# Another order of the projected tiles in a fused gated-delta-rule and feed-forward block

## The chip, the cores and the metric

The kernel runs on one core of one Trainium2 chip. The metric is the device time of one execution in microseconds (us). The kernel before takes 1098.72 us, the median of three runs (1098.14 to 1103.36).

## What is computed

Four sequences of 512 tokens, width 512. Each half is modulated by a condition (layer norm, scale, shift, gate). The first half is a gated delta rule with 6 heads (key 64, value 128), the second a SiLU-gated feed-forward of 2048. All in f32.

```python
h = _layernorm(x) * (1 + ca) + sa
q = short_conv(h @ Wq, conv_wq)      # 384 columns; conv over 4 tokens, then silu
k = short_conv(h @ Wk, conv_wk)      # 384 columns
v = short_conv(h @ Wv, conv_wv)      # 768 columns
beta = sigmoid(h @ Wb); g = -exp(A_log) * softplus(h @ Wa + dt_bias)
# per token: S = S*exp(g); S += k (v - k S) beta; o = q S
o = o * rsqrt(mean(o*o) + EPS) * norm_weight * silu(h @ Wg)   # gate: 768 columns
x = x + ga * (o @ Wo)
x = x + gb * ffn(_layernorm(x) * (1 + cb) + sb)
```

## The kernel before, in words

The host-side code first writes a plan, a list of steps in one order; each engine then walks that list and issues its own part of every step, so all engines share the plan's order, and waits are semaphores. The stages are: norms and the projection of k (4 x 4 slots, to about 90 us); the projection of q, v and the output gate, beside which the inverses for the chunks are made (to about 338 us); a recurrence over 16 units (to about 540 us); the feed-forward.

The change is in the second stage. It has 15 tiles of 128 columns, three of q (numbers 0 to 2), six of v (3 to 8) and six of the gate (9 to 14); `tile_seq` is their order. Each tile is done for 4 batches, so there are 60 slots. In the prediction a projection or taps "of slot n" carry the slot's number, from 0. In slot n:

- TensorE first projects for slot n+1: 12 matmuls of 128x512, the f32 product being made of three products of float32r halves (L1258 is the helper that issues a matmul). It needs one of four PSUM banks, freed by the slot four before.
- At the first slot of a tile the next tile's weights are split: high part on ScalarE, difference ("weight difference") on VectorE (L1851 is the helper for all tensor_tensor operations), and the load of a later weight on SyncE's queue waits for that difference.
- q or v tile ("convolution slot"): `conv_in` on ScalarE scales the bank into one of two Y buffers; `conv_out` on ScalarE, one slot late, writes SiLU of Y into one of three output buffers O; three `conv_tap` operations on VectorE ("taps", L1956), of which the last frees the bank. Gate tile ("gate slot"): one SiLU on ScalarE from the bank into an O buffer, which frees the bank. `store_u` on SyncE's queue (L1131) stores O to `scrU` in DRAM.
- Then the side lanes put in their next steps. L1580 is the helper for every ScalarE activation.

The side lanes, with the steps that matter:

- `inverse_1`, from slot 4: per group of four units a table load, exponentials, a table load back; per unit a product k·k on TensorE and one VectorE operation (L2022), two copies on ScalarE, and four stores to `scrA` on SyncE (L1138).
- `inverse_2`, once all 16 units are planned: loads from `scrA` (L1148), then the substitution: 31 pairs of a multiply and an add on VectorE, each needing the one before; then stores to `scrP` (L1162), 16 loads back (L1169) that wait for these stores, and the P tiles being cleared on GpSimd (L2265). The lane makes three steps in a gate slot and at most two in a convolution slot.
- `q_norms`, from slot 21: loads of q, squares on ScalarE in slots 28 to 30, sums and turns on TensorE in slots 32 and 33.
- `merge`, once the loads back are planned: per unit 12 small products (merge_a), copies on ScalarE, transposes on VectorE (L2067), 12 more (merge_b) and copies on VectorE (L2056). TensorE's steps use two pairs of PSUM banks in turn.

In the kernel before the loads from `scrA` are in slot 15, the substitution in slots 17 to 41, the stores to `scrP` in slot 42, the loads back in slot 44, the merges in slots 46 to 55.

```python
            else:
                step("conv_in", j=3 + tile, bank=i, done=t, y=y, n=ys["n"], tap=tap)
                put_out()
                for k in range(3):
                    step("conv_tap", j=3 + tile, bank=i, y=y, tap=tap, d=k)
                left[1] = min(left[1], 2)
```

Of the kernel before, what the change touches and what calls it, by code (L numbers as in the profile page):

```python
# [53 lines left out]
def build(nc, x, W1, cw, dtb, alog, nw, Wo, cT, wmod, wg, cst, out):  # L54
# [212 lines left out]
        return ap.unsqueeze(axis).broadcast_to(shape)  # L267

    order = [s * 4 + b for b in range(4) for s in range(4)]
    tile_seq = [0, 9, 1, 10, 2, 11, 3, 12, 4, 13, 5, 6, 7, 8, 14]  # L270
    MODS = [0, 1, 3, 2, 4, 5]
    WSEQ = [0, 1, 2, 3] + [4 + n for n in tile_seq]

# [2134 lines left out]
```

How the kernel before makes its waits and increments, by code:

```python
    def all_posted(e):  # L1056
        e.wait_ge(sem("po_wo"), 16)
        e.wait_ge(sem("p_x1"), 16)
        e.wait_ge(sem("v_xn1"), 16)
        for n in range(2):
            e.wait_ge(sem(f"d_x1{n}"), 512)
# [17 lines left out]
    def sync(e):  # L1079
        def load_x(n):
            u = order[n]
            if n >= 5:
                e.wait_ge(sem("v_xn"), n - 4)
            e.dma_start(X[n % 5][:, :], x[u % 4, (u // 4) * 128:(u // 4) * 128 + 128, :]).then_inc(sem(f"d_x{n % 5}"), 16)
# [1 line left out]
        def load_mod(r):  # L1086
            i = MODS[r]
            if r >= 2:
                e.wait_ge(sem("mod_mm"), r - 1)
            if r == 0:
                e.dma_start(wm[0][:, 0:2, :], wmod[:, 0:2, i * 512:(i + 1) * 512]).then_inc(sem("d_wmh"), 16)
                e.dma_start(wm[0][:, 2:4, :], wmod[:, 2:4, i * 512:(i + 1) * 512]).then_inc(sem("d_wm0"), 16)
                return
            e.dma_start(wm[r % 2][:, :, :], wmod[:, :, i * 512:(i + 1) * 512]).then_inc(sem(f"d_wm{r % 2}"), 16)
# [1 line left out]
        def load_w(j):  # L1096
            if j >= 2:
                e.wait_ge(sem("v_wlo"), j - 1)
            e.dma_start(Wraw[j % 2][:, :, :], W1[WSEQ[j]]).then_inc(sem(f"d_w{j % 2}"), 16)
# [28 lines left out]
            elif kind == "store_u":  # L1128
                o, b = st["o"], st["b"]
                e.wait_ge(*at_least(st["act"]))
                e.dma_start(scrU.rearrange("(s b) p j t -> b j p s t", b=4)[b, st["tile"]],
# [2 lines left out]
                u = st["u"]  # L1134
                s, w = unit(u)
                e.wait_ge(sem("v_ab6"), u + 1)
                for k in range(4):
```

## Time and profile before

| | |
|---|---|
| median of three runs | 1098.72 us |
| profiled execution | 1101.88 us |
| its span, first to last instruction | 1099.9 us |
| mean granted TensorE clock | 0.983 |
| TensorE matmul / weight load busy | 95% / 77% |
| VectorE / ScalarE / GpSimd busy | 57% / 34% / 19% |
| projection of q, v, gate, with the inverses | about 90 to 338 us |

The profile is of one execution. Busy shares are means over stages with different limits. Matmuls overlap in the array and their ends are modelled, so that TensorE can seem busy where it runs with short waits. "PEld" is the weight load, "SPq" SyncE's queue of DMA issues. A value in brackets behind a row is the idle time of the engine ahead of it and what ended it. The granted clock is a share of 2.4 GHz.

### The profile page before, as it was taken

To read this page: it belongs to the slowest core of one execution; us is meant where nothing else is said; L and a number is where in the kernel's file an instruction comes from. 1 tells how busy PE (TensorE), PEld (TensorE's weight loads), DVE (VectorE), ACT (ScalarE), POOL (GpSimd) and SP (SyncE) were. 2 spreads that over 40 slices of the span, in tenths; PEclk is the share of its full clock that TensorE was granted. 3 is DMA by queue.
4 is the path that set the end of the run, shared out by engine and by line. 5 is a ranking of instruction groups with operands and counts; after the bars stand their busy time and mean duration, and the time that the engine had idled before them with its cause. 6 is when DMAs were issued, how large, how long until landed. Compare 5 with 4: busy or idle time off the path is not lost.

```text
span 1099.9 us, 18621 instructions
## 1 busy us (share of the span) xinstructions
PE 1046.9 (95%) x7356; PEld 844.7 (77%) x7356; DVE 632.2 (57%) x995; ACT 374.3 (34%) x685; POOL 207.8 (19%) x163
## 2 busy tenths in 40 slices
PE   5799999998989999999989999999999999999998
PEld 3675667777767788888777787888888888888886
DVE  6868355999774677787766333333333433434356
ACT  3476464353445333343355112121221211122110
POOL 1132200011014544544331000000000000004191
PEclk8899999999889999999999999999999999999999
DMA  6503235737519466666622000010010100001223
GB/s 218 181 10 119 69 79 155 214 96 197 97 49 228 93 143 136 158 166 139 207 79 77 1 1 29 29 33 25 1 57 1 58 1 29 29 1 67 77 77 115
DMA packets 153414, 97.34 MB, mean 89 GB/s; under 512 B 93552, under 2 KB 130672, under 8 KB 153200
## 3 DMA queue, kind: packets, MB, share of 16 engines
q1 hardware_dynamic: 153328, 96.16, 32.2%
q8 instruction: 59, 0.97, 0.4%
q14 instruction: 27, 0.22, 0.1%
HBM read 64.67 MB, written 31.46 MB: 87 GB/s over the span
## 4 chain that ended last, share of the span: by engine, by line
PE 77%; DVE 12%; issue 4%; ACT 2%; DMA 2%; SPq 2%; POOL 1%; DVEq 0%; ACTq 0%; POOLq 0%
PE ps L1258 73%; DVE t L1851 5%; DVE t L1956 3%; PE ps L1266 3%; ACT t L1580 2%; DVE t L1856 1%; PE ps L1463 1%; DMA t<-in_x 1%; DMA t<-scrA 1%; SPq L1138 1%; DVE t L1861 1%; SPq L1195 1%; POOL t L2244 0%; DMA t<-scrU 0%; DVE t L2056 0%
## 5 line engine op out<-in xcount | busy, mean ns | idle before, releaser
L1258 PE MATMUL ps<-t,t 128*128 128x512 f32 (+6 forms) x6488 | 995.4, 338 | 42.3 <-DVE t L1851 16.8
L1258 PEld LDWEIGHTS ps<-t,t 128*128 128x128 f32 (+4 forms) x6488 | 787.0, 166 | 227.4 <-issue 45.1
L1851 DVE TENSOR_TENSOR t<-ps,t 128x512 f32<-128x512 f32 (+4 forms) x306 | 208.2, 700 | 257.9 <-PE ps L1258 243.6
L1580 ACT ACTIVATE t<-t 128x512 fp32r<-128x512 f32 (+10 forms) x339 | 188.8, 578 | 326.8 <-DVE t L1851 201.5
L1851 DVE TENSOR_TENSOR t<-t,t 128x512 fp32r<-128x512 f32 (+15 forms) x212 | 166.9, 792 | 109.2 <-ACT t L1580 98.2
L1580 ACT ACTIVATE t<-ps 128x512 f32<-128x512 f32 (+5 forms) x202 | 108.9, 551 | 317.2 <-PE ps L1258 308.7
L2334 POOL TENSOR_TENSOR t<-t,t 128x512 f32<-128x512 f32 x16 | 22.4, 1401 | 375.2 <-DVE t L1851 373.1
L1956 DVE SCALAR_TENSOR_TENSOR t<-ps,t,t 128x511 f32<-128x511 f32 (+2 forms) x108 | 80.3, 747 | 8.9 <-ACT t L1580 6.1
L1266 PE MATMUL ps<-t,t 128*128 128x128 f32 (+1 forms) x388 | 54.7, 276 | 5.0 <-DVE t L1856 2.8
L1580 ACT ACTIVATE t<-ps,t 128x512 f32<-128x512 f32 (+2 forms) x93 | 54.5, 616 | 14.0 <-PE ps L1266 6.7
L1266 PEld LDWEIGHTS ps<-t,t 128*128 128x128 f32 (+1 forms) x388 | 43.1, 142 | 16.5 <-issue 5.3
L2313 POOL TENSOR_TENSOR t<-t,t 128x768 fp32r<-128x768 f32 x16 | 29.1, 1818 | 42.9 <-ACT t L1580 42.7
L2265 POOL MEMSET t<- 128x3072 f32 x4 | 10.7, 2671 | 124.8 <-PE ps L1258 97.5
L2319 POOL TENSOR_TENSOR t<-t,t 128x512 f32<-128x512 f32 x16 | 20.7, 1296 | 55.6 <-DVE t L1851 55.4
L1580 ACT ACTIVATE t<-t,t 128x1 f32<-128x1 f32 (+2 forms) x36 | 13.2, 368 | 52.8 <-DVE t L1863 51.5
L2337 POOL TENSOR_TENSOR t<-t,t 128x512 f32<-128x512 f32 x16 | 22.9, 1430 | 39.9 <-DMA t<-scrX 37.9
L1861 DVE BATCH_NORM_STATS2 t<-t 128x6 f32<-128x512 f32 x32 | 22.0, 689 | 10.3 <-DMA t<-in_x 8.5
L2244 POOL TENSOR_TENSOR t<-t,t 128x512 fp32r<-128x512 f32 x13 | 17.0, 1304 | 52.8 <-ACT t L1580 51.5
L1856 DVE TENSOR_SCALAR t<-t,t,t 128x512 f32<-128x512 f32 x32 | 25.1, 787 | 3.1 <-PE ps L1266 2.9
L1944 DVE SCALAR_TENSOR_TENSOR t<-ps,t,t 128x510 f32<-128x510 f32 (+1 forms) x24 | 17.8, 744 | 11.5 <-ACT t L1580 10.9
L2305 POOL TENSOR_TENSOR t<-t,t 128x768 f32<-128x768 f32 x16 | 23.6, 1472 | 2.7 <-POOL t L2319 2.4
L2255 POOL TENSOR_TENSOR t<-t,t 128x384 f32<-128x384 f32 x16 | 13.7, 858 | 52.3 <-PE ps L1258 32.8
(50 smaller groups left out, 236.7 us busy)
## 6 DMA issues: line engine op xcount, KB each, us to landing
scrU<-t SPq DMA_DIRECT2D x60, 256.0 KB, 3.2
t<-in_wf SPq DMA_DIRECT2D x16, 768.0 KB, 4.2
t<-scrU SPq DMA_DIRECT2D x32, 288.0 KB, 4.7
t<-scrU SPq DMA_DIRECT2D x32, 192.0 KB, 3.4
t<-in_wmod SPq DMA_DIRECT2D x5, 1024.0 KB, 6.2
t<-in_W SPq DMA_DIRECT2D x19, 256.0 KB, 3.0
t<-in_x SPq DMA_DIRECT2D x16, 256.0 KB, 4.3
t<-in_x SPq DMA_DIRECT2D x32, 128.0 KB, 2.8
```

The lines of the kernel that those rows point to most:

```text
L1258: return e.matmul(o, l, r_, start=start, stop=stop, skip_group_check=True)
L1266: return e.transpose(o, i, idn)
L1580: return e.activation(o, i, f, **kw)
L1851: return e.tensor_tensor(o, a, b, op)
L1856: return e.tensor_scalar(o, a, s1, s2, o1, o2)
L1861: e.bn_stats(st6[:, slot_, :], src).then_inc(sem(name + "bn"), 1)
L1956: e.scalar_tensor_tensor(yy[:, d + 1:SEQ], p_[:, 0:SEQ - d - 1], cwt[:, j, 2 - d:3 - d], yy[:, d + 1:SEQ], ALU.mult, ALU.add).then_inc(sem ...
L2305: signal(e.tensor_tensor(heads(Sg[:, :, :]), heads(S[:, 6 * pp:6 * pp + 6, :]), bc(decay, 3, [128, 2, 3, 128]), ALU.mult), "p_sg")
L2313: signal(e.tensor_tensor(OZl[:, :, :], OZ[:, :, :], OZh[:, :, :].bitcast(f32), ALU.subtract), "p_ozl")
L2319: signal(e.tensor_tensor(YB[u % 2][:, :], YB[u % 2][:, :], XB[u % 2][:, :], ALU.add), "p_x1")
L2334: signal(e.tensor_tensor(ya(b, s), ya(b, s), gbB[:, b, :], ALU.mult), "p_out")
L2337: signal(e.tensor_tensor(ya(b, s), ya(b, s), xo(b, s), ALU.add), "p_out")
```

## The change

One line of the plan is another. Tile numbers 0 to 2 are q, 3 to 8 v, 9 to 14 gate.

```diff
     order = [s * 4 + b for b in range(4) for s in range(4)]
-    tile_seq = [0, 9, 1, 10, 2, 11, 3, 12, 4, 13, 5, 6, 7, 8, 14]
+    tile_seq = [0, 9, 1, 2, 3, 10, 11, 12, 13, 4, 5, 6, 7, 8, 14]
     MODS = [0, 1, 3, 2, 4, 5]
     WSEQ = [0, 1, 2, 3] + [4 + n for n in tile_seq]
```

Slots 0 to 11 and 40 to 59 keep their tiles. Slots 12 to 19 are q2 and v3, slots 20 to 35 four gate tiles, slots 36 to 39 v4. As the substitution's lane makes three steps in a gate slot and two in others, its last step comes in slot 40 instead of 41; the stores to `scrP` come in slot 41 instead of 42, the loads back in slot 42 instead of 44, and the merges in slots 45 to 54 instead of 46 to 55. The loads of the weights follow the new order.

## Rows read from the trace of the kernel before

**Rows 1.** The page: busy time of TensorE and share of the span.
```profile
span 1099.9 us, 18621 instructions
...
PE 1046.9 (95%) x7356; PEld 844.7 (77%) x7356; DVE 632.2 (57%) x995; ACT 374.3 (34%) x685; POOL 207.8 (19%) x163
```

**Rows 2.** Chain of waits, 126 to 350 us: start, length, what.
```profile
175.94 3.17 DMA scrA<-t
...
180.02 7.26 DMA t<-scrA
...
246.09 24.77 PE ps L1258 x108
270.87 3.74 issue
```

**Rows 3.** Busy time by stretch: stretch, length, engines, clock, DMA share, GB/s.
```profile
187.30:246.00 58.70, 53.72 (x264) 40.56 (x262) 56.88 (x79) 25.26 (x51) 5.35 (x2) 1.00 0.53 152
```

**Rows 4.** Timeline of TensorE, 160 to 300 us: start, length, what, [idle before].
```profile
190.22 22.31 PE L1258 MATMUL ps<-t,t 128*128 128x512 f32 x96 [2.10 <-DVE t L1956]
213.42 3.06 PE L1258 MATMUL ps<-t,t 128*128 128x512 f32 x12 [0.89 <-DVE t L1956]
...
226.05 16.03 PE L1258 MATMUL ps<-t,t 128*32 128x512 f32 x104 [0.15 <-ACT t L1580]
...
274.61 1.49 PE L1258 MATMUL ps<-t,t 32*32 32x32 f32 x48 [3.74 <-issue]
...
283.17 8.42 PE L1258 MATMUL ps<-t,t 32*32 32x32 f32 x168 [0.48 <-ACT t L1580]
```

**Rows 5.** Busy time by stretch of one microsecond; the third number from the end is the clock.
```profile
274.00:275.00 1.00, 0.39 (x15) 0.42 (x17) 0.43 (x2) 0.00 (x0) 0.00 (x0) 0.60 1.27 150
...
280.00:281.00 1.00, 1.00 (x3) 0.76 (x3) 0.86 (x3) 0.00 (x0) 0.00 (x0) 0.50 0.68 89
...
295.00:296.00 1.00, 1.00 (x4) 0.81 (x3) 0.93 (x3) 0.00 (x0) 0.00 (x0) 0.50 0.48 131
```

**Rows 6.** Timeline of VectorE, 126 to 262 us.
```profile
144.19 2.32 DVE L1956 SCALAR_TENSOR_TENSOR t<-ps,t,t 128x511 f32<-128x511 f32 x3 [1.83 <-ACT t L1580]
...
149.27 2.31 DVE L1956 SCALAR_TENSOR_TENSOR t<-ps,t,t 128x511 f32<-128x511 f32 x3 [1.81 <-ACT t L1580]
...
173.18 0.56 DVE L2022 SCALAR_TENSOR_TENSOR t<-ps,t 128x384 f32<-128x384 f32 x1 [1.33 <-DMA scrA<-t]
...
261.37 0.54 DVE L1851 TENSOR_TENSOR t<-t,t 128x93 f32<-128x93 f32 x2
```

**Rows 7.** Timeline of ScalarE, slots 12 and 48.
```profile
162.69 1.28 ACT L1602 ACT_TABLE_LOAD   x1
163.99 1.64 ACT L1580 ACTIVATE t<-ps 128x384 f32<-128x384 f32 x4
...
285.72 0.62 ACT L1580 ACTIVATE t<-t 128x512 f32<-128x512 f32 x1
```

**Rows 8.** Timeline of the SyncE queue, 160 to 300 us.
```profile
172.44 3.94 SPq L1138 DMA_DIRECT2D scrA<-t  x8
...
179.16 1.29 SPq L1148 DMA_DIRECT2D t<-scrA  x3
...
262.61 2.19 SPq L1162 DMA_DIRECT2D scrP<-t  x3
...
269.03 11.15 SPq L1169 DMA_DIRECT2D t<-scrP  x16
```

**Rows 9.** VectorE's groups by form, 186 to 262 us: count, busy, mean ns.
```profile
L1851 DVE TENSOR_TENSOR t<-t,t 128x512 fp32r<-128x512 f32 x6 | 4.1, 685 | 0.0
...
L1851 DVE TENSOR_TENSOR t<-t,t 128x768 f32<-128x768 f32 x2 | 1.9, 958 | 0.1
...
L1851 DVE TENSOR_TENSOR t<-t,t 128x93 f32<-128x93 f32 x4 | 1.1, 276 | 5.2 <-DMA t<-scrA 5.1
```

**Rows 10.** DMA issues, 160 to 355 us: KB each, median us to landing.
```profile
scrU<-t SPq DMA_DIRECT2D x49, 256.0 KB, 3.2
```

## The prediction

> **What bounds the kernel now.** I read the page first, then the chain of waits of the projection stage, then the timelines of TensorE, VectorE, ScalarE and the SyncE queue there, and last the granted clock in stretches of one microsecond. The page puts the kernel on TensorE: 95% busy [rows 1]. Only order changes, and only in slots 12 to 39, so what can be won or lost is TensorE's waiting, and time at the lower clock, between about 150 and 340 us; everything behind shifts with it. A slot is one 128-column tile for one batch; there are 60. TensorE runs a slot's projection one slot ahead, and can run up to three ahead, for four banks.
>
> The chain shows what waited last, in this order [rows 2]. Early TensorE; then the SyncE queue that stores the inverse's blocks, a landing, and the load of the substitution's operand, done at 187.3. Then VectorE until 246; TensorE again, 24.77 us for nine projections, 2.75 each; then 3.74 us in which TensorE stands for the inverse's return from memory. In 187.3 to 246 VectorE is busy 56.88 of 58.70 us, but TensorE 53.72 [rows 3]. TensorE's waits are few: 2.10 before 190.22 and 0.89 before 213.42, with some 2 us more at two like places; it makes eight projections in 22.31 us, 2.79 each, while VectorE is behind [rows 4]. The four banks absorb most of VectorE's lateness.
>
> The clock: at the higher level (1.00, 2.4 GHz) until 274, 0.60 in 274 to 275, 0.50 (1.2 GHz) until 281 and then 1.00 again [rows 5]. It follows the 3.74 us wait. Some 6.8 us at half rate lose 3.4 us. It falls three times more, first at 295 [rows 5], some 3.4 us each, each losing 1.7; these follow slots with four small merges.
>
> **The change part by part.** Instructions, bytes and buffers are the same. Tiles q1, q2, v3 stand in slots 8 to 19, gates in 20 to 35, v4 in 36 to 39. Against before, slots 12-15 become convolution slots, 24-27 and 32-35 gates, 36-39 a convolution; 16-23 and 28-31 keep their kind (with other tiles). Between the arrival of the substitution operand and its last sum stand five convolution slots fewer: before 18, 19, 24-27, 32-35, 40, 41 and after 18, 19, 36-40.
>
> Step 1, the head. In slots with a convolution and two unit products, VectorE's taps start every 5.08 us (144.19 to 149.27) [rows 6]: taps 2.24 (2.32 with the overlap at their end), products 1.05, then on ScalarE the copies of the blocks (1.5) ahead of the next slot's scaling, then 0.72 to the taps. In gate slots before, unit 15 is done at 173.18 + 0.56 = 173.7 [rows 6]. After: taps of 12 at 161.2, product 11 at 164.0, copy to 164.8, two table loads of 1.28 around 1.64 us of exponentials [rows 7] to 169.0, taps of 13 at 169.7, of 14 at 174.8, unit 15 done at 178.1: 4.4 late. The queue then has eight stores of 0.49 each to issue [rows 8], so the last starts at 181.0 instead of 175.9; 3.2 to land, and 8.1 from the first load's issue (179.16) to arrival at 187.3: **192.3, 5 us late**. Meanwhile ScalarE and VectorE have done slots 15 to 17, and these wait no longer than before. The SyncE queue holds the stores of 15 to 17 and a weight load behind this wait; the three output buffers cover that, as each is asked for after 190.
>
> Step 2. VectorE does one multiply (0.28) [rows 9], then the taps of slot 18, to 194.9, and only that frees a bank. By my bank-by-bank count TensorE has finished projection 21 at 190.7 (before 188.1; 2.3 us of it for a buffer that product 11 frees later) and stands 4.3 us instead of 2.1.
>
> Step 3. That is longer than the 3.74 us that the clock did not outlast, so I charge a fall: from the first projection behind the stand (274.61 + 1.49 of small merges, one more of 0.6: 276.8 [rows 4]) to 281 it took some 4 us, at half rate 1.8 to 2; I take 1.8. Bounds 0 and 3.4, the row's whole loss.
>
> Step 4, the gates. Slots 20 to 35 hold 48 substitution steps, each 0.28 to 0.96 by its size, 38.6 us summed over the grouped rows of which the ends stand here, and four weight differences of 0.685 [rows 9]: 41.3 on VectorE. TensorE needs 16 x 2.79 plus 4.8 for the norm sums of slots 32 and 33 (16.03 with four projections of 2.8 [rows 4]): 49. So TensorE bounds it and VectorE's 7 us spare is no gain on the path. Projection 36 is done at 195.0 + 4.55 + 2.75 + 13 x 2.79 + 4.8 = 243.4, before 239.2.
>
> Step 5. Slots 36 to 40 are VectorE's again: 243.4 + 0.72, five taps groups 11.2, the last steps 3.7, a weight difference 0.7: last sum at 259.7; before 261.37 + 0.54 = 261.9 [rows 6]. **2.2 us early.**
>
> Step 6. Store to loads to first merge takes what it took: 0.7, then 6.4 (262.61 to 269.03) and 5.6 to 274.61 [rows 8, 4]. First merge at 272.4, 2.2 early. But the merges start in slot 45 instead of 46, so one projection more (2.75) is left: **0.5 us slower** by here. TensorE's wait is 1.5 instead of 3.7.
>
> Step 7, who stands behind the moved loads. The 16 loads back stand in slot 42 of the queue, not 44: two output stores earlier. They occupy SyncE for 11.15 us [rows 8]; every store from slot 43 on waits to 266.8 + 11.15 = 278.0. Output buffers are three, so the SiLU in slot 46 waits for the store from slot 43, 3.2 to land [rows 10]: 281.2. Before, the one that had to wait was in slot 48: free at 280.2 + 3.2 = 283.4, reached at 285.7 [rows 7], no wait. Now ScalarE would be there at 275, before the copies of merges 2 and 3. TensorE gets to 278.5 (1.5 of merges, 0.6, a projection, 1.2), then stands until 281.2 + 0.63 + 0.67 = 282.5, and has slot 46's merges done at 283.7 with projection 47. Before had slot 47's done at 283.17 + 0.6 = 283.8 [rows 4], with projection 48. So 283.7 + 2.75 - 283.8 = **+2.7 us**; the old fall's 3.4 us are in the time before and are not charged to the new one. A stand of 4.0 us may drop the clock once more, 1.8; I charge half: **+3.6 us**. Against the profiled execution (1101.88; its span 1099.9) that is 1105.5; the median of the runs lies 3.2 lower, 1098.72, and there it is **1102.3**.
>
> A rule read against this: the TensorE row here is 95% busy for matmuls and 77% for weight loads [rows 1], and in 187.3 to 246 it is 92% and 69% [rows 3]. The Trainium skill, Perfetto Trace Analysis, Identifying the Most-Contended Engine, says that matmul busy is no good measure of closeness to the limit, and that the engine of highest occupancy is to be optimized. By it VectorE at 97% is the bound of this stretch, and the sum would be the first rival's; by my bank count it would not.
>
> **The rivals.** A, VectorE bounds all of 187 to 262, and five groups of taps taken out are worth their 5 x 2.24 = 11.2 us. Start 5 late, so the substitution ends 6.2 early; less one projection 2.75, and the wait and its fall of clock shrink: 6.2 - 2.75 + 3.4 = 6.9 faster, 1091.8. For it speaks the busy share; against it that TensorE, at 2.75 a slot, can't give 16 gates in 41 us.
>
> B, no new stand matters: the clock does not fall at 195 (-1.8), the output buffer comes free in time, the old fall vanishes (-3.4): 0.5 - 1.8 - 3.4 = 4.7 faster, 1094.0. For it: the wait of 3.74 goes down. Against: the three buffers and the 11.15 us.
>
> C, slower: the stand for the output buffer decides. It costs as soon as the loads back end later than 3.2 us before ScalarE reaches slot 46, that is after 272; each microsecond more is one on the path. With the store landing in 4.9, as the last store to scrP does (264.1 to 269.03 [rows 8]), rather than 3.2, the second fall in full, and one more fall in the merges: 3.6 + 1.7 + 0.9 + 1.7 = 7.9 slower, 1106.6.
>
> D, the order doesn't take effect on the substitution: excluded by the plan, since the rate of two steps beside a convolution and three beside a gate follows from the slot's kind; counted under the forecast.
>
> **How the numbers follow.** Forecast 0.56, A 0.12, B 0.16, C 0.16. A measurement of this kernel tells about 0.5%, 5.5 us, from no change. Faster by more: A, and the quick end of B: 0.15. Slower by more: C and the slow end of the forecast (both falls in full): 0.23. Same 0.62. The range takes in B and C, and nearly A: 1093.0 to 1107.5.
>
> **What would show it.** The operand's landing near 192 instead of 187.3; TensorE's wait of about 4 us there, and 0.5 in the clock just behind; TensorE without waits from 197 to 243 while VectorE idles; last sum near 260; first merge near 272; ScalarE's wait for a store (scrU) at 275 to 281. Wrong if VectorE stays busy through the gates, if the clock stays at 1.00 at 195, or if the SiLU of slot 46 finds its buffer.

## The result and the profile after

The changed kernel takes 1104.93 us, the median of 14 runs (1101.88 to 1106.68); the kernel before, over as many, 1099.28. The ratio is 1.0042 (95% interval 1.0031 to 1.0052): 4.6 us slower, where 3.6 had been forecast. The ratio is estimated over all the runs; the two medians lie 5.65 us apart. The change is within the 0.5% that the prediction called no change, and clear of noise at this number of runs.

The page answers to [rows 1]. Work is the same; the span of the profiled execution grew from 1099.9 to 1103.4 us.

```profile
span 1103.4 us, 18621 instructions
...
PE 1050.1 (95%) x7356; PEld 848.9 (77%) x7356; DVE 633.4 (57%) x995; ACT 374.2 (34%) x685; POOL 207.9 (19%) x163
```

This execution was 0.86 us behind the earlier one before the orders differ (the fourth unit's product, L2022, starts at 133.06 instead of 132.20). The lines and the times in this section are as the profile has them; where the account of the prediction, further down, sets the two side by side, 0.86 is taken off.

The chain of waits, answering to [rows 2], start, length, what:

```profile
187.92 0.76 DVE t L1956
...
189.50 53.24 PE ps L1258 x260
...
260.70 6.46 DMA scrP<-t
267.18 0.32 SPq L1169
...
278.39 3.04 DMA scrU<-t
281.45 0.84 ACT t L1580 x2
...
282.68 7.32 PE ps L1258 x106
```

VectorE's long stretch of the chain, 187 to 246 before, is now TensorE's for 53 us. What came in its place stands lower: the 16 loads back (L1169), then one output store (scrU), then ScalarE. Before, no store was in the chain here.

Timeline of TensorE, answering to [rows 4]: in brackets the idle time ahead (a "stand" below) and what ended it.

```profile
164.88 6.59 PE L1258 MATMUL ps<-t,t 128*128 128x384 f32 x20 [2.06 <-DVE t L2022]
...
189.50 80.43 PE L1258 MATMUL ps<-t,t 128*128 128x512 f32 x380 [2.25 <-DVE t L1956]
272.05 0.95 PE L1258 MATMUL ps<-t,t 32*32 32x32 f32 x48 [2.11 <-issue]
...
282.68 11.04 PE L1258 MATMUL ps<-t,t 32*32 32x32 f32 x168 [4.98 <-ACT t L1580]
```

The short waits between 190.3 and 246 are gone: one piece of 80.43 us. Three stands are new or in another place: 2.06, 2.25 and 4.98 us. The 3.74 ahead of the first merge is 2.11.

Busy time by stretch, answering to [rows 3, 5]; the third number from the end is the granted clock.

```profile
166.00:170.00 4.00, 4.00 (x12) 2.98 (x11) 0.00 (x0) 3.94 (x7) 0.00 (x0) 0.58 0.18 31
187.30:246.00 58.70, 56.49 (x276) 44.62 (x277) 53.87 (x74) 24.06 (x50) 5.34 (x2) 0.97 0.66 193
...
190.00:191.00 1.00, 1.00 (x4) 0.81 (x3) 0.93 (x3) 0.86 (x2) 0.00 (x0) 0.50 0.96 365
...
278.00:279.00 1.00, 0.00 (x0) 0.00 (x0) 0.91 (x4) 0.00 (x0) 0.00 (x0) 1.00 0.13 16
...
284.00:285.00 1.00, 1.00 (x3) 0.81 (x4) 0.71 (x3) 0.97 (x3) 0.00 (x0) 0.50 0.00 1
...
296.00:297.00 1.00, 1.00 (x25) 0.94 (x26) 0.82 (x3) 0.71 (x2) 0.00 (x0) 0.50 0.00 0
```

In 187.3 to 246 VectorE is busy 53.87 us instead of 56.88, and TensorE loads weights for 44.62 instead of 40.56. The clock is at half (1.2 GHz) four times: about 166 to 170 (1.7 us lost, summed over stretches of one microsecond as one less the clock), 189 to 194 (1.7), 282 to 289 (3.4) and 295 to 303 (3.4). Before it was 3.4 at 274 to 281 and three times 1.7 later.

VectorE, answering to [rows 6]:

```profile
183.78 2.62 DVE L2029 MEMSET t<- 128x3072 f32 x1 [0.59 <-issue]
...
187.15 4.53 DVE L1956 SCALAR_TENSOR_TENSOR t<-ps,t,t 128x511 f32<-128x511 f32 x6
...
196.88 21.02 DVE L1851 TENSOR_TENSOR t<-t,t 128x180 f32<-128x180 f32 x28
220.25 22.69 DVE L1851 TENSOR_TENSOR t<-t,t 128x512 fp32r<-128x512 f32 x27 [2.34 <-ACT t L1580]
243.49 2.31 DVE L1956 SCALAR_TENSOR_TENSOR t<-ps,t,t 128x511 f32<-128x511 f32 x3 [0.55 <-ACT t L1580]
...
258.42 0.25 DVE L1851 TENSOR_TENSOR t<-t,t 128x93 f32<-128x93 f32 x1
```

The first row is the fill of the substitution's result tile. The two rows of L1851 with 28 and 27 operations are the gates' stretch; the waits that the profile shows in and behind it are 2.34 and 0.55 us. The last sum ends at 258.7.

ScalarE and the SyncE queue, answering to [rows 7, 8]:

```profile
219.03 0.60 ACT L1580 ACTIVATE t<-ps 128x512 f32<-128x512 f32 x1 [5.28 <-DMA scrU<-t]
...
281.45 0.63 ACT L1580 ACTIVATE t<-t 128x512 f32<-128x512 f32 x1 [6.73 <-DMA scrU<-t]
```

```profile
184.43 1.30 SPq L1148 DMA_DIRECT2D t<-scrA  x3
...
259.65 2.19 SPq L1162 DMA_DIRECT2D scrP<-t  x3
261.89 1.18 SPq L1131 DMA_DIRECT2D scrU<-t  x1
267.18 11.16 SPq L1169 DMA_DIRECT2D t<-scrP  x16
278.39 0.53 SPq L1131 DMA_DIRECT2D scrU<-t  x1
```

From 267.18 to 278.35 the queue issues loads; the store that has to free a buffer is issued at 278.39, and ScalarE's SiLU of slot 46, there from 274.7, starts at 281.45.

### The profile page after: what moved, and what is told of

Same layout as the page of the kernel before. It is cut to its first block, busy times and chain, and to the rows that moved or that the text cites. A ratio compares the mean times of both kernels' runs of the same rounds, so it can differ in the third digit from the quotient of the medians.

```text
span 1103.4 us, 18621 instructions
## 1 busy us (share of the span) xinstructions
PE 1050.1 (95%) x7356; PEld 848.9 (77%) x7356; DVE 633.4 (57%) x995; ACT 374.2 (34%) x685; POOL 207.9 (19%) x163
## 4 chain that ended last, share of the span: by engine, by line
PE 78%; DVE 9%; ACT 4%; issue 4%; DMA 2%; SPq 2%; POOL 1%; DVEq 0%; ACTq 0%; POOLq 0%
PE ps L1258 74%; ACT t L1580 3%; PE ps L1266 3%; DVE t L1956 3%; DVE t L1851 3%; DVE t L1856 1%; SPq L1169 1%; PE ps L1463 1%; DMA t<-in_x 1%; DMA scrP<-t 1%; ACT L1602 1%; DMA scrU<-t 1%; SPq L1195 1%; DMA t<-scrU 1%; DVE t L1861 0%
## 5 line engine op out<-in xcount | busy, mean ns | idle before, releaser
L1851 DVE TENSOR_TENSOR t<-ps,t 128x512 f32<-128x512 f32 (+4 forms) x306 | 208.3, 700 | 257.9 <-PE ps L1258 243.2
L1851 DVE TENSOR_TENSOR t<-t,t 128x512 fp32r<-128x512 f32 (+15 forms) x212 | 167.7, 796 | 107.7 <-ACT t L1580 103.4
L1861 DVE BATCH_NORM_STATS2 t<-t 128x6 f32<-128x512 f32 x32 | 22.1, 689 | 10.2 <-DMA t<-in_x 8.4
```

Of the source, the lines that this page charges most:

```text
L1851: return e.tensor_tensor(o, a, b, op)
L1861: e.bn_stats(st6[:, slot_, :], src).then_inc(sem(name + "bn"), 1)
```

## The experiments

All ratios are to the kernel before, timed on the same chip; 0.1% is 1.1 us. Experiments 1 to 4, 5 to 8, and 9 and 10 ran on three different chips, so two experiments are compared by their ratios and not by their times.

**1. The loads back spread.** The changed order; other steps come between the loads.

```diff
         for s in range(4):
             step("inv2_back", s=s, cleared=cleared[s])
-        for _ in range(3):
-            yield
+            if s < 3:
+                yield
```

> The changed kernel, but its 16 loads back from scrP go into the plan four at a time (slots 42, 43, 43, 44) instead of all in slot 42, so that output stores stand between them. Theory 1 (most of the loss is the stand behind these loads): ScalarE no longer waits 6.7 us for an output buffer at 275 to 281, TensorE's stand of 4.98 us ahead of 282.7 goes, and the half-rate stretch from 282 to 288.4 (3.2 us lost) with it; 5 to 8 us faster than the changed kernel, so 1097 to 1100 us, level with the kernel before or under it. Theory 2 (the loss is in the head, slots 12 to 19, and the merges would drop the clock anyway, as they did three times before): at most 2 us faster, 1102 to 1105.

Measured: 1099.0 us, ratio 0.9992 (0.9977 to 1.0006). Against 1.0042 that is 0.50%, 5.5 us: theory 1. The queue, and ScalarE where the wait of 6.73 us had been:

```profile
268.32 2.03 SPq L1169 DMA_DIRECT2D t<-scrP  x4
270.39 0.53 SPq L1131 DMA_DIRECT2D scrU<-t  x1
271.01 4.82 SPq L1169 DMA_DIRECT2D t<-scrP  x8
```

```profile
274.85 0.69 ACT L1580 ACTIVATE t<-ps,t 128x512 f32<-128x512 f32 x1
275.44 0.62 ACT L1580 ACTIVATE t<-t 128x512 f32<-128x512 f32 x1
281.05 0.67 ACT L1580 ACTIVATE t<-ps 32x192 f32<-32x192 f32 x2 [4.99 <-PE ps L1258]
```

The SiLU (275.44) follows the scaling at once. TensorE's stand of 4.98 us is gone. But the clock still falls, at 273 to 281 (3.4 lost), now with the first merges, after a stand of 1.59; theory 1 had it gone. In this profile the next fall, at 294 to 298, costs 1.7 where the changed kernel lost 3.4 at 295 to 303. How the 5.5 us divide between the stand and the clock is open: in 150 to 345 us the two profiles lose nearly the same to half rate (10.1 and 10.2), but over all executions the mean granted clock is 0.984 here and 0.980 in the changed kernel, a difference worth 4.5 us over the span.

**2. The fills on GpSimd.** The changed order; the zeros and the diagonal of ones are written by GpSimd, with the same waits (the added lines below are in GpSimd's part; the diagonal's lines are left out).

```diff
             elif kind == "inv2_load":
-                e.wait_ge(sem("v_gn"), 10)
-                e.wait_ge(sem("v_turn"), 4)
-                e.memset(Pp[:, :, :, :], 0.0).then_inc(sem("v_fill"), 1)
...
+            elif kind == "inv2_load":
+                e.wait_ge(sem("v_gn"), 10)
+                e.wait_ge(sem("v_turn"), 4)
+                in_order()
+                signal(e.memset(Pp[:, :, :, :], 0.0), "p_fill")
...
```

> The changed kernel, but the two fills of the substitution's result tile (2.62 us on VectorE at 183.8) are done by GpSimd, which is idle there. Theory: that fill, which I had left out of my count, is what holds the taps of slot 16 and with them TensorE at 187.25 to 189.50 and the clock behind. Without it the taps of slots 15 to 17 are done at about 189 instead of 191.7, TensorE's stand shrinks from 2.25 to about 0.6 us, ahead of projection 22, and no half-rate stretch follows: 2 to 3.5 us faster than the changed kernel, the later parts shifted as a whole. Rival: the operand's arrival (about 191) holds slot 18 anyway and TensorE stands there just as long: under 0.7 us.

Measured: 1103.13 us, ratio 1.0029 (1.0016 to 1.0041), 1.4 us less than the change; the two intervals overlap, so the time alone doesn't show a gain. The trace has something of the theory and something of the rival:

```profile
184.41 4.53 DVE L1956 SCALAR_TENSOR_TENSOR t<-ps,t,t 128x511 f32<-128x511 f32 x6
192.10 0.26 DVE L1851 TENSOR_TENSOR t<-t,t 128x93 f32<-128x93 f32 x1 [3.16 <-DMA t<-scrA]
```

```profile
194.64 24.91 PE L1258 MATMUL ps<-t,t 128*128 128x512 f32 x108 [1.11 <-DVE t L1956]
```

The taps come 2.7 us earlier, in an execution that is itself 0.8 us later, and TensorE doesn't stand at 187; nor does the clock fall there. But VectorE then waits 3.16 us for the operand, and half of the 2.25 us comes back as a stand of 1.11 us at 194.6.

**3. The loads spread in the kernel before**, a control.

> The kernel before with its loads back spread in the same way (slots 44, 44, 45, 45). A control: in that kernel the SiLU behind these loads was reached at 285.7 with its buffer free at 283.4, so both theories expect no change, within 1 us of the kernel before. A gain of 3 us or more would mean that spreading helps in itself (the loads arriving otherwise), not by the stores behind them.

Measured: 1100.25 us, ratio 1.0011 (0.9996 to 1.0026). No gain. In this kernel, where nobody waited for the stores behind the loads, spreading them is worth nothing; in the changed one it is worth 5.5 us.

**4. The gates alone.**

```diff
-    tile_seq = [0, 9, 1, 10, 2, 11, 3, 12, 4, 13, 5, 6, 7, 8, 14]
+    tile_seq = [0, 9, 1, 10, 2, 11, 12, 13, 3, 4, 5, 6, 7, 8, 14]
```

> Another order that does only the second half of the change: q, gate, q, gate, q as before, then three gate tiles (slots 20 to 31), then v3 and v4 (32 to 39). The head (slots 12 to 15) stays a gate tile, and the loads back stay in slot 44. If gates beside the substitution were worth anything where VectorE is 97% busy, this is 3 to 7 us faster than before. By my count TensorE bounds the gates at 2.79 a slot and VectorE the ten convolution slots after them at 3.9, so it is within 2 us of before, the waits of 0.9 us between 212 and 246 being moved, not removed.

Measured: 1101.0 us, ratio 1.0003 (0.9988 to 1.0018). Gathering the gates is worth nothing by itself. The experiment says less about VectorE than its text supposes: by the plan 13 convolution slots (17 to 19 and 32 to 41) still lie beside the substitution, as many as before (17 to 19, 24 to 27, 32 to 35, 40, 41), so no taps were taken from it. Experiment 6 and the changed kernel do take some away. TensorE:

```profile
189.20 54.50 PE L1258 MATMUL ps<-t,t 128*128 128x512 f32 x272 [0.50 <-DVE t L1956]
244.85 3.06 PE L1258 MATMUL ps<-t,t 128*128 128x512 f32 x12 [1.15 <-DVE t L1956]
...
274.50 1.16 PE L1258 MATMUL ps<-t,t 32*32 32x32 f32 x48 [4.69 <-issue]
```

The short waits moved from 212 to 246 to 244 to 259 (the first of them is shown), and the stand ahead of the merges grew from 3.74 to 4.69: with 0.57 taken off, by which this execution was late at the fourth unit, TensorE is done with its projections 1.6 us earlier than before and the first merge comes only 0.7 earlier. The 0.50 ahead of 189.20 is not the order's doing: six profiles have the same tiles up to slot 19 (before and experiments 3, 4, 8, 9, 10), and this stand is 2.10, 0.50, 0.50, 0.77, 1.49 and 2.52 us in them. It goes with the operand's way through memory: from the start of VectorE's last product (L2022) to its first multiply (L1851) they took 14.13, 12.55, 12.54, 12.84, 13.50 and 14.59 us.

**5. Both edits of 1 and 2** on the changed kernel.

> The changed kernel with both edits, the loads back spread and the fills on GpSimd. If the two losses are separate (5.5 us and 1.4 us by the runs of each alone, against the changed kernel), the sum is 6.9 us: 1098 us or a ratio of 0.998 to the kernel before. If the earlier merges of one run into the stand of the other, under 5.5.

Measured: 1098.76 us, ratio 0.9981 (0.9967 to 0.9996): 0.61% under the change, 6.7 us, where 6.9 was the sum. That fits two separate losses; against experiment 1 alone the gain is 1.2 us with overlapping intervals. What is left of the change by itself is slightly faster than before.

**6. The head alone**, with the loads spread as in 1.

```diff
-    tile_seq = [0, 9, 1, 10, 2, 11, 3, 12, 4, 13, 5, 6, 7, 8, 14]
+    tile_seq = [0, 9, 1, 2, 10, 11, 3, 12, 4, 13, 5, 6, 7, 8, 14]
```

> An order that does only the first half of the change: q2 in slots 12 to 15, then gate, gate, v3, gate, v4, gate (slots 16 to 39), with the loads back spread as in the run before, so that no store stands behind them. Theory of the prediction (the head costs its stands: 2.06 us for a pair of banks at 164.9 and a later operand, less the 2.10 that was there before, and two falls of the clock of 1.7): 2 to 5 us slower than before, 1101.5 to 1104.5. Rival (the convolutions done early are given back later, since VectorE then has four fewer beside the substitution): within 1 us of before.

Measured: 1100.79 us, ratio 0.9997 (0.9979 to 1.0015), within 1 us of before, as the rival had it. The stand at 164 is there, and the fall at 164 to 169 too:

```profile
164.31 6.65 PE L1258 MATMUL ps<-t,t 128*128 128x384 f32 x20 [2.05 <-DVE t L2022]
...
273.36 1.04 PE L1258 MATMUL ps<-t,t 32*32 32x32 f32 x48 [2.43 <-issue]
```

But the stand ahead of the first merge is 2.43 instead of 3.74, and that merge starts at 273.4, not 274.6: four convolution slots were done before the substitution could start. Their taps are 9.0 us of VectorE's work (4 x 2.24), and the kernel is no faster for it.

**7 and 8. TensorE kept at work ahead of the merges.** Matmuls whose results nobody reads, one step ahead of the first merge: 8 on the kernel with both edits, 14 on the kernel before.

```diff
+            elif kind == "warm":
+                e.wait_ge(*at_least(st["free"]))
+                for k in range(8):
+                    mm(bank(4 + 2 * st["p"]), Hhi[:, 0, k % 4, 0:128], Hhi[:, 0, k % 4, :], True, True)
```

> As the kernel with both edits, and before the first merge TensorE makes 8 matmuls of 128x512 whose results nobody reads (extra work, into the bank that the merge overwrites), in the 1.6 us in which it stands there. They take 1.8 us. If the stand ahead of the small merges is what drops the clock at 273 (3.4 us lost in 273 to 281), the clock stays at 1.00 there and this is 2 to 3.4 us faster than with both edits. If the small merges themselves do it, it falls all the same, and this is level or 0.3 us slower.

Measured: 1097.53 us, ratio 0.9968 (0.9954 to 0.9982).

> The kernel before with 14 such matmuls (extra work, not read, 3.2 us) in its stand of 3.74 us at 270.9 ahead of the first merge. If the stand drops the clock there, 3.4 us (the loss in 274 to 281) come back: 1096, a ratio of 0.997. If not, no change.

Measured: 1099.22 us, ratio 0.9987 (0.9972 to 1.0001). The stretches in question, first with 8 on both edits, then with 14 on the kernel before, where [rows 5] had 0.50:

```profile
273.00:274.00 1.00, 1.00 (x26) 0.87 (x21) 0.55 (x2) 0.95 (x3) 0.00 (x0) 1.00 1.07 159
...
280.00:281.00 1.00, 1.00 (x6) 0.84 (x5) 0.96 (x2) 0.63 (x1) 0.00 (x0) 1.00 0.84 133
```

```profile
277.00:278.00 1.00, 1.00 (x15) 0.83 (x8) 0.73 (x3) 0.98 (x3) 0.00 (x0) 1.00 1.49 129
280.00:281.00 1.00, 0.92 (x49) 0.74 (x48) 0.94 (x4) 0.32 (x1) 0.00 (x0) 1.00 0.79 56
```

The clock stays at 2.4 GHz through the first merges in both. So the first merges by themselves don't drop it; what does in the falls from 291 us on, among merges with no stand above 1.3 us, is open. With unread matmuls it holds there in three profiles of three (these and experiment 10); without them it falls within 2 us of the first merge's start in eight of nine, behind stands of 1.59 to 4.69 us. In the ninth, the changed kernel, it holds at the first merges after 2.11 us and falls behind the 4.98. The gain in time is not shown: it is 1.4 us each, against experiment 5 and against the kernel before, where up to 3.4 had been expected; the first has overlapping intervals, and the interval of the second reaches 1.0001. In these two executions 3.4 and 1.7 us are lost to half rate in 150 to 342 us, against 6.8 in the profile of experiment 5, and 8.5, 6.8 and 5.1 in those of the kernel before and its two controls (3 and 9). Falls come and go between executions, and both profiled ones are among the fastest of their kernels (1096.42 and 1097.76 us).

**9. The fills on GpSimd in the kernel before**, a control.

> The kernel before with the two fills on GpSimd: a control. There VectorE stood idle when the fill came (gate slots), so if the fill costs only where it stands ahead of taps that TensorE waits for, this is level with the kernel before, within 1 us. A gain of 1.4 us as in the changed kernel would mean that the gain has nothing to do with the head of the changed order.

Measured: 1100.23 us, ratio 0.9999 (0.9986 to 1.0013). No gain, as expected: here the fill costs nothing.

**10. Gates alone, fills moved, 18 unread matmuls.** A miss.

> The order with gates alone (q2 in slots 16 to 19, gates in 20 to 31, v3 and v4 in 32 to 39), the fills on GpSimd, and 18 unread matmuls (4.1 us) in the stand of 4.69 us ahead of its first merge. If the stand there was worth its half-rate stretch of 3.4 us, 1.5 to 3.5 us faster than this order by itself (1.0003): a ratio near 0.998, as good as the kernel with the loads spread. If the earlier start of the merges in that kernel is what counts, it stays at 0.9985 or above.

Measured: 1103.35 us, ratio 1.0022 (1.0003 to 1.0040), slower where faster was expected. The clock holds at the first merges (1.00 through 275 to 293), but TensorE stands 2.52 us ahead of 190.46 instead of the 0.50 of experiment 4, and the clock falls there and three times in the merges:

```profile
190.46 55.94 PE L1260 MATMUL ps<-t,t 128*128 128x512 f32 x272 [2.52 <-DVE t L1962]
...
276.37 0.95 PE L1260 MATMUL ps<-t,t 32*32 32x32 f32 x48 [0.56 <-issue]
```

The first merge comes at 276.4 instead of 274.5. This execution had the longest way of the operand through memory among the six with this head (14.59 us, see experiment 4), and the stand of 2.52 goes with it; the kernel before had 14.13 and 2.10. That is one execution. Why the whole series is slower is open: its runs spread wider (1098.4 to 1108.4) than any other kernel's, and its interval overlaps that of experiment 4, so the loss is shown against the kernel before but not against the same order by itself.

## Why the prediction was right

The median of the longer series lies 2.6 us above the predicted time and well within the range; the direction was right. By its steps; 0.86 is taken off a time of the profile after where it stands beside a predicted one or one of before:

**Step 1, right but for one instruction.** Unit 15 was to be done at 178.1; VectorE's last product pair ends at 178.03 + 1.02 = 179.05, less the 0.86 of this execution 178.2. Left out was the fill of the result tile, 2.62 us on VectorE, which the plan issues with the load in slot 15. In the kernel before it ran at 174.3 to 176.9, and VectorE still waited 5.09 us for the operand behind it; in the new order it stands ahead of taps that TensorE waits for. The prediction's list of what moves with the load counted its transfers and not its VectorE part. The operand came sooner than 192.3: where VectorE waits for it (experiment 2) it is there at 192.1 in an execution 1.7 us late, so at 190.4, 3.1 us after the 187.3 of before and not 5. The 8.1 us from the first load's issue to arrival that the prediction took over were on the long side; experiments 3 and 4 have 7.1.

**Step 2, wrong place, half the size.** The stand was 2.25 us ahead of projection 20, not 4.3 ahead of 22. The 2.10 of before, with which it was compared, is itself a matter of the execution (0.50 to 2.52 in six profiles). Another stand, 2.06 us at 164.9, for the pair of banks behind product 11, was in the count (2.3) but not charged with a fall of the clock.

**Step 3, right in size, not in place or reason.** The clock fell at 189 to 194 for 1.7 us of loss (1.8 charged), behind the shorter stand. At 195 it was back at 1.00, which the prediction had named as a sign of being wrong. Its reason, a stand longer than 3.74 us, did not come about: 2.25 us was enough here and 2.16 in experiment 1, while 2.10 in the kernel before was not. The clock also fell at 166 for another 1.7, behind 2.06 us. That fall is in all six profiles with q2 in slots 12 to 15 (the change and experiments 1, 2, 5, 6, 7) and in none of the six without.

**Step 4, right in the bound, wrong in the spare.** Projection 36 ended at about 241.9 (243.4 predicted) and TensorE had no wait of note in 80 us, against rival A. VectorE's spare was not 7 us but waits of 2.34 and 0.55: it began the stretch later (the fill), and waited for ScalarE, whose gates stood for output buffers while the queue issued q loads, a weight load and other stores (5.28 us ahead of 219.03). By here TensorE was 1.5 us earlier than forecast.

**Steps 5 and 6, right in order, 1 to 2 us late.** Last sum at 257.8 (259.7), first merge at 271.2 (272.4), stand ahead of it 2.11 (1.5). By here the prediction had the change 0.5 us slower. By the profile it is 0.7 faster: the first merge is 3.4 us earlier than the 274.61 of before, less one projection of 2.75. Experiment 1, which leaves steps 1 to 6 alone, says 0.9 us faster with an interval from 2.5 faster to 0.7 slower. Experiments 4 and 6, a part of the new order each, come out level.

**Step 7, right in mechanism, time and place.** SiLU of slot 46 at 280.6 (281.2), TensorE back at 281.8 (282.5), its stand 4.98 (4.0). Spreading the loads, which removes it (experiment 1), is worth 5.5 us, all of the loss and a little more. Mis-sized was the clock behind it: 0.9 charged, 3.4 lost in 281 to 289. In part that is a moved stretch: where the stand is gone the same 3.4 are lost at the first merges. The term of the sum as a whole, 2.7 + 0.9 = 3.6 from 0.5, so 3.1, against the 5.5 measured, is the one that made the forecast short.

**The rivals.** A falls. With five groups of taps (11.2 us) out and the operand 3.1 us late, the last sum should have come 8.1 us earlier if VectorE were the bound; it came 4.1 earlier, while TensorE ran 80 us without a wait. Without the stand for the buffer (experiment 1) the whole is 0.9 us faster and not 6.9, and with four groups out (experiment 6) it is level. The rule of the Trainium skill that the prediction quoted (Perfetto Trace Analysis, Identifying the Most-Contended Engine: optimize the engine of highest occupancy) pointed at VectorE in this stretch, which the prediction worked out as 6.9 us; the measurement decides against it here. TensorE's own idle time in 187.3 to 246 was 4.98 us (58.70 less 53.72 [rows 3]); by these rows that is the most idle time that relieving VectorE could give back in the stretch. B is what experiment 5 comes to, 2.1 us under the kernel before instead of 4.7. C is the same mechanism at a larger price, and of its three surcharges two came: the second fall in full, and 1.7 more lost in the merges (3.4 at 295 to 303 for 1.7 before). The third, a slower store, did not (3.04 us). Its 7.9 us is still further from the 4.6 measured than the forecast's 3.6, as the profile after has no fall from 303 to 342 where the one before had two of 1.7.

What the forecast's size owes to luck: everything up to the first merge was put 1.4 us too slow (0.5 slower, where experiment 1 says 0.9 faster), and step 7 was put 2.4 us too small (3.1 for 5.5). These partly cancel, and 1.0 us is left. Within the first part, too, the missing fill (1.4 us by experiment 2, not clear of noise) stands against an operand forecast 1.9 us too late.

## What to carry to other kernels

When a plan is reordered, follow every instruction of the moved step on every engine and queue, and then who stands behind it: here 16 loads two slots earlier in one in-order queue kept a store from issuing, a three-buffer ring ran out, and 5.5 us were lost, while the reordering itself was worth at most some 2 us. An engine at 97% beside one at 92% is not yet what bounds the stretch; first count the idle time of the other one, which is all that can be won there. Spread a burst of issues over the plan where somebody waits for what stands behind it. Unread matmuls in a stand ahead of small work kept the clock up in three profiles; that they gain time is not shown.

## What the hardware showed unexpectedly

The clock of TensorE was at half rate for stretches that lose 1.7 or 3.4 us, nothing between, at 150 to 340 us in all profiles here. It fell behind stands of 2.06 and 2.25 us (166 and 190), shorter than the 3.74 us of the kernel before from which the prediction argued; behind a stand of 1.59 us and small merges it fell too (experiment 1), and behind 0.49 us and the same merges it did not (experiment 7). The same order ahead of the merges lost 8.5, 5.5 and 5.1 us in three executions (before, experiments 3 and 9), so a difference of some 3 us between single profiles of these kernels says nothing.
